# Delta-rule stage of an audio tower: squares on the off-diagonal tiles, two groups' products in one TensorE job, 16 slots instead of 28

## The reference, cut to what matters

```
qkvb = (normed @ W_slow.T).reshape(slen, bsz, H, 5 * D + 2)       # slen 64, bsz 246, H 8, D 64
q, k, v, rk, rv, beta, rbeta = jnp.split(qkvb, ...)
q, k, rk = softmax of each;  beta, rbeta = sigmoid of each
def fw_step(W, inp):                                              # one step of the first recurrence
    qt, kt, vt, bt = inp
    v_old = jnp.einsum('bhij,bhj->bhi', W, kt)
    W = W + (bt * (vt - v_old))[..., :, None] * kt[..., None, :]
    return (W, jnp.einsum('bhij,bhj->bhi', W, qt))
```

## Time and profile before

| what | us |
|---|---|
| time of the kernel, median of 3 runs | 18280.08 (18266.01 to 18282.9) |
| profiled execution, first to last instruction (span) | 18228.0 |
| stage `delta`, first to last instruction | 5642.9 to 9888 of the span |
| PE busy, of the span | 13070.7 (72%) |
| DVE / ACT / POOL busy, of the span | 10572.6 / 6554.5 / 2261.8 |

### The profile page before, as it was taken

The page is one execution under the profiler, slowest core; times in us unless marked ns, Lnnn a source line. Parts: engine busy times, 40 slices in busy tenths (PEclk is TensorE's granted clock), DMA queues, the critical chain, the costliest instruction groups (busy, mean ns, idle before and its releaser), DMA issues. The chain is left out here.

```text
span 18228.0 us, 593330 instructions
## 1 busy us (share of the span) xinstructions
PE 13070.7 (72%) x262069; PEld 10252.8 (56%) x262069; DVE 10572.6 (58%) x24424; ACT 6554.5 (36%) x16019; POOL 2261.8 (12%) x1394
## 2 busy tenths in 40 slices
PE   4607778770866999999997766776677676867777
PEld 3504566660544777777775555555555565645555
DVE  6451457774125666666666777666767645446664
ACT  3101236550213666666664221111112122345541
POOL 0038200003461111111111000000000000000001
PEclk9556568875867999999998766776687697967775
DMA  0313320121332111111112112201220152177652
GB/s 20 110 26 49 72 48 21 34 76 33 72 59 67 28 25 27 28 26 27 27 26 51 21 38 45 44 19 38 45 44 19 38 149 79 45 237 195 193 135 65
DMA packets 1835030, 1095.27 MB, mean 60 GB/s; under 512 B 1109166, under 2 KB 1763409, under 8 KB 1814481
## 3 DMA queue, kind: packets, MB, share of 16 engines
q1 hardware_dynamic: 1605063, 999.32, 22.7%
q0 software_dynamic: 227328, 57.19, 2.1%
HBM read 569.43 MB, written 484.53 MB: 58 GB/s over the span
## 5 line engine op out<-in xcount | busy, mean ns | idle before, releaser
L2894 PE MATMUL recur_acc<-recur_U,recur_W 8*32 8x64 f32 (+4 forms) x49152 | 1406.2, 270 | 504.8 <-ACT recur_W L2816 429.9
L2894 PEld LDWEIGHTS recur_acc<-recur_U,recur_W 8*32 8x32 f32 (+4 forms) x49152 | 1071.1, 140 | 924.5 <-ACT recur_W L2816 741.8
L2945 DVE TENSOR_TENSOR recur_pr<-recur_K,recur_e 124x64 f32<-124x64 f32 (+60 forms) x1024 | 1282.0, 1252 | 395.8 <-ACT recur_e L2828 395.6
L2881 PE MATMUL recur_acc<-recur_R,recur_E 128*32 128x64 f32 x62976 | 1212.6, 233 | 243.2 <-issue 232.7
L2950 DVE TENSOR_REDUCE recur_dot<-recur_pr 124x1 f32<-124x64 f32 (+60 forms) x1024 | 1281.6, 1252 | 29.7
L2881 PEld LDWEIGHTS recur_acc<-recur_R,recur_E 128*32 128x32 f32 x62976 | 1078.3, 118 | 343.5 <-issue 288.1
L2816 ACT ACTIVATE recur_W<-recur_wT 128x256 f32<-128x256 f32 (+16 forms) x1024 | 336.1, 328 | 1969.9 <-PE recur_wT L2866 1968.8
L2866 PE MATMUL recur_wT<-const_ident,recur_w 128*128 128x128 f32 (+15 forms) x1536 | 480.8, 375 | 768.5 <-DVE recur_w L2954 762.1
L2475 ACT ACTIVATE delta_B1l<-delta_pS 64x256 f32<-64x256 f32 x1968 | 745.1, 379 | 704.5 <-PE delta_pS L2375 679.9
L2475 ACT ACTIVATE delta_B0l<-delta_pS 64x256 f32<-64x256 f32 x1968 | 745.6, 379 | 620.9 <-PE delta_pS L2375 600.5
L2510 POOL TENSOR_TENSOR delta_QK<-delta_QK,delta_mx 128x512 f32<-128x512 f32 x369 | 380.3, 1045 | 3038.1 <-DVE delta_mx L2563 3038.0
(11 more groups left out here) (620 smaller groups left out, 33946.8 us busy)
## 6 DMA issues: line engine op xcount, KB each, us to landing
scr<-rel_BD SPq DMA_DIRECT2D x128, 1288.0 KB
rel_sc<-scr SPq DMA_DIRECT2D x128, 861.0 KB
xnT<-ln_xT SPq DMA_DIRECT2D x64, 492.0 KB, 3.0
kr<-delta_QK SPq DMA_DIRECT2D x492, 64.0 KB, 2.3
ur<-delta_Uf SPq DMA_DIRECT2D x492, 64.0 KB, 2.2
zz<-delta_Z SPq DMA_DIRECT2D x492, 64.0 KB, 2.2
recur_K<-kr SPq DMA_DIRECT2D x64, 448.0 KB
recur_H<-zz SPq DMA_DIRECT2D x64, 448.0 KB
```

The lines of the kernel that those rows point to most:

```text
L2881: nc.tensor.matmul(acc[a][32 * q:32 * q + 32, 0:FD], E[a][:, EQ * q + 32 * j:EQ * q + 32 * j + 32], R[a][:, m, :], start=(j == 0), stop=False)
L2894: ins = nc.tensor.matmul(acc[a][32 * q:32 * q + 32, 0:FD], W[a][0:8 * k, b, 160 * q + 32 * j:160 * q + 32 * j + 32], U[a][0:8 * k, 2 * (t ...
L2945: V.tensor_tensor(pr[0:cp, 0:n, :], K[a][0:cp, r0:r0 + n, :], e[a][0:cp, None, :].to_broadcast([cp, n, FD]), ALU.mult).then_inc(s_own[a], 1)
```

## The change

- In `job(one, two)`, which replaces `head`, `tail` and `outer`, the squared transpose goes to the off-diagonal tiles too (into `pS`, now two kinds side by side, 64 columns each), and the applied part alone stays on the diagonal tiles (into `pM`). The tail or the outer product of another group is issued in the same loop, on the diagonal tiles. All products have 64 columns. `outer` of group G - 1 stands in the job of level 3, k = 0.
- A group has 8 jobs, a pair 16 slots, numbered without the empty places. The last slots of a run have tails alone.
- ACT copies both kinds of `pS` at once: two copies of 64 partitions x 512 (64 x 256 at the last level) instead of three copies, and doesn't wait for DVE there.
- The projections stand at slots 0 to 4, each behind that slot's job. The two of values are no longer copied by ACT: DVE scales them from PSUM into a double buffer `V0`, at slots 3 and 4. The other three copies stand in the projection's own slot instead of the next.
- Maxima at slots 1 to 3 (before 2 to 4), exponentials at 3 to 5 (before 5 to 7), sums at 5 to 7 (before 7 to 9), transposes at 8 to 10 (before 16 to 18).
- The key products of both groups go into two PSUM buffers at once, on all four tiles, in three sets (slots 11, 13, 15) instead of six; their masks stand at slots 11 to 15, and set 2 and 3 wait for the masks of the set before.

```diff
-        NM, NG_, NE, NV = 10, 14, 8, 4
-        PROJ_AT = {0: 0, 1: 1, 2: 2, 11: 3, 12: 4}
-        TURN_AT = {16: 0, 17: 1, 18: 2}
-        GRAM_AT = {19: 0, 20: 1, 21: 2, 22: 3, 23: 4, 24: 5}
-        MAX_AT, EXP_AT, SUM_AT = 2, 5, 7
+        NM, NG_, NE, NV = 10, 11, 6, 4
+        NSLOT = 16
+        PROJ_AT = {0: 0, 1: 1, 2: 2, 3: 3, 4: 4}
+        VAL_AT = {3: 0, 4: 1}
+        MAX_AT, EXP_AT, SUM_AT = 1, 3, 5
+        TURN_AT = {8: 1, 9: 2, 10: 0}
+        GRAM_AT = {11: 0, 13: 1, 15: 2}
+        MASK_AT = {11: ((0, 0),), 12: ((0, 1),), 13: ((1, 0),), 14: ((1, 1),), 15: ((2, 0), (2, 1))}
...
-                        for a in range(4):
-                            for h in HALF:
-                                mm(pM[k][h, a, more.start - 1:2, :], now[h, a, 0, :], now[h, a, more, :])
-                            for x, h in enumerate(HALF):
-                                ins = mm(pS[k][HALF[1 - x], a, :], now[h, a, 1, :], now[h, a, 0, :])
...
+                        for a in range(4):
+                            for x, h in enumerate(HALF):
+                                if one and l < SQ - 1:
+                                    mm(pS[k][HALF[1 - x], a, 1, :], now[h, a, 0, :], now[h, a, 1, :])
+                                if one:
+                                    done_one = mm(pM[k][h, a, :], now[h, a, 0, :], u[h, a, :])
+                            for x, h in enumerate(HALF):
+                                if one:
+                                    done_one = mm(pS[k][HALF[1 - x], a, 0, :], now[h, a, 1, :], now[h, a, 0, :])
+                                if two and kind == "tail":
+                                    last = level(k2, G2 % 2, SQ)
+                                    done_two = mm(pT[k2][h, a, :], last[h, a, 0, :], P[k2][h, a, :] if m else last[h, a, 2, :])
+                                elif two:
+                                    done_two = mm(pT[0][h, a, :], az[G2 // 2 % 2][G2 % 2][h, a, :], P[0][h, a, :])
...
                         if n in TURN_AT:
...
+                            if j < 2:
+                                pe.wait_ge(s_v, NV * p + 2 * j + 2)
+                            else:
+                                pe.wait_ge(s_e, NE * p + 4)
                             if j == 0:
                                 pe.wait_ge(s_k, p + 1)
...
                         if n in GRAM_AT:
+                            kind = GRAM_AT[n]
+                            if kind == 0:
+                                pe.wait_ge(s_e, NE * p + 6)
+                            else:
+                                pe.wait_ge(s_m, NM * p + 4 * kind)
                             for a in range(4):
+                                for g in range(2):
+                                    for h in HALF:
+                                        ins = mm(gp[g][h, a * FD:(a + 1) * FD], ...)
...
+                            kinds = slice(0, 2) if l < SQ - 1 else slice(0, 1)
                             for x, h in enumerate(HALF):
-                                ins = nc.scalar.activation(new[h, :, 0, :], pS[k][HALF[1 - x], 0:4, :], ACT.Copy)
-                            if l < SQ - 1:
-                                act.wait_ge(s_dv[k], SQ * G + l + 1)
-                                ins = nc.scalar.activation(new[:, :, 1, :], pM[k][:, :, 0, :], ACT.Copy)
+                                ins = nc.scalar.activation(new[h, :, kinds, :], pS[k][HALF[1 - x], :, kinds, :], ACT.Copy)
                             ins.then_inc(s_ac[k], 1)
...
+                            for g in range(2):
+                                V.tensor_tensor(V0[(p + newer) % 2][k][:, g], vv[:, g], be[:, g].unsqueeze(2).to_broadcast([128, 4, FD]),
+                                                ALU.mult).then_inc(s_v, 1)
```

More of the change, by code:

```diff
@@ L2358, in entries @@
                     for k in range(2):
-                        order.append((G // 2, 14 * (G % 2) + len(order) % 14, ("head", G, x, k)))
-                        if x < TL:
-                            order.append((G // 2, 14 * (G % 2) + len(order) % 14, ("tail", G - 1, x, k) if G else None))
+                        second = None
+                        if G and x < TL:
+                            second = ("tail", G - 1, x, k)
+                        elif G and k == 0:
+                            second = ("outer", G - 1, x, k)
+                        order.append((G // 2, 8 * (G % 2) + 2 * x + k, (G, x, k), second))
             for x in range(TL):
                 for k in range(2):
-                    order.append((pairs, 28, ("tail", 2 * pairs - 1, x, k)))
+                    order.append((pairs, NSLOT, None, ("tail", 2 * pairs - 1, x, k)))
+            order.append((pairs, NSLOT, None, ("outer", 2 * pairs - 1, TL, 0)))
             return order
         def step_of(base, solves, preps):
-            work = entries(solves) if solves else [(0, n, None) for n in range(28)]
+            work = entries(solves) if solves else [(0, n, None, None) for n in range(NSLOT)]
+            newer = 1 if solves else 0
+            rhs = lambda G, l, k: V0[G // 2 % 2][k][:, G % 2] if l == 0 else level(k, G % 2, l)[:, :, 2, :]
             with st.step() as block:
@@ L2427, in _ @@
                     xv = xc[:].rearrange("p a s -> p (a s)")
                     kt = lambda kind, hd: KT[FD * (hd % 2):FD * (hd % 2) + FD, 4 * kind + hd // 2, :]
-                    for p, n, job in work:
-                        if job is not None:
-                            kind, G, x, k = job
-                            (head if kind == "head" else tail)(G, x, k)
-                            if kind == "head" and x == SQ - 1 and k == 0 and G:
-                                outer(G - 1)
-                            if n == 28 and x == TL - 1 and k == 1:
-                                outer(G)
+                    for p, n, one, two in work:
+                        if one or two:
+                            job(one, two)
@@ L2518, in read_head @@
                     def read_head(G, l, k):
[L2519 removed]
+                        u = rhs(G, l, k)
                         dve.wait_ge(s_S[k], SQ * G + l + 1)
@@ L2541, in read_outer @@
                         V.tensor_copy(Z[:, :, G % 2, :], pT[0][:, 0:4, :]).then_inc(s_z, 1)
-                    for p, n, job in work:
+                    for p, n, one, two in work:
                         if n == 0 and p < preps:
-                            new = base + p + (solves > 0)
+                            new = base + p + newer
                             V.tensor_copy(xc[:].rearrange("p a s -> p s a"), X[:, :, bass.ds(2 * new, 2)]).then_inc(s_x, 1)
@@ L2550, in _ @@
                             V.tensor_copy(sb_[p % 2][:], beta[:, bass.ds(new, 1)].rearrange("p n h a -> p (n h) a")).then_inc(s_be, 1)
-                        if job is not None:
-                            kind, G, x, k = job
-                            (read_head if kind == "head" else read_tail)(G, x, k)
-                            if kind == "head" and x == SQ - 1 and k == 1 and G:
-                                read_outer(G - 1)
-                            if n == 28 and x == TL - 1 and k == 1:
-                                read_outer(G)
+                        if one:
+                            read_head(*one)
+                        if two and two[0] == "tail":
+                            read_tail(*two[1:])
+                        elif two:
+                            read_outer(two[1])
                         if p >= preps:
```

137 lines of the change are left out of this document (56 added, 81 removed).

## The result

The changed kernel takes **18642.61 us** (median of 4 runs, 18626.67 to 18645.54), the kernel before 18281.49 beside it (18266.01 to 18284.57): a ratio of 1.0194, 95% interval [1.0181, 1.0206]. It is slower by 361 us; 146 were forecast. The direction, the gap and the fall of the clock came as predicted.

What follows compares the result with a forecast made beforehand. PE's queue was taken to bound the stage, busy 30.99 of 33.10 us a round. 32.1 at full clock plus 2.2 for the clock gave 34.3, 1.2 more x 122 = 146 us: 18425 us, range 18140 to 18750.

Steps and rivals of the forecast that it cites:

- the sum of the round at full clock: New round added slot by slot with PE at full clock: 31.5 us plus 0.6 for seams, 32.1.
- the correction for seams: Old round's priced parts came to 31.7 us, 1.4 under the 33.1 measured; half, 0.6, was added to the new round.
- The clock's term: Half-rate PE work behind each round's gap adds 1.5 to 2.8 us a round, middle 2.2.
- rival 1: Clock holds through each round's gap: -1.0 us a round, 18160; 18050 if DVE reaches the last sum 1.5 sooner; chance 0.19.
- Slots 0 to 4, 2.09 us each: Job 0.93, shape change 0.10 and projection 1.06 in each of the first five slots; ACT and DVE hide.
- The ACT pair, 1.20: ACT's two 512-wide copies reading a job take 2 x 0.60 us, bounds 0.98 to 1.3.
- The chain sum, scales, scaling, transposes: From last sum at 14.84 us, 1.57 to POOL's start, 2.76 scaling, keys ready 19.2, slot 8's transposes start 19.27.
- A gap of 3.5 to 4.5 us released by the scaling: PE idles 4.0 us a round, 15.23 to 19.27, before slot 8's transposes, until POOL's scaling of the keys ends.
- The gap throttles the clock, through J9 or J10: Each round's gap sends PE to 1.2 GHz, at half rate through slot 9's or 10's job; stage clock 0.75 to 0.92.
- Rival 2: Clock stays down until the next round's projections: +7.2 us, 19035; 18650 if down to slot 12 or so; chance 0.16.
- Rival 3: Packing doesn't pay, a job takes 1.33 to 1.39 us: round 35.7 without clock effect, 18597; chance 0.05.
- Rival 4: Both effects cancel, clock falling only in some rounds or for one job: round 33.1, 18280; chance 0.10.

Runs made afterwards that it cites:

- w1: Changed kernel with five full-array products of 256 columns, results unused, put in PE's gap ahead of slot 8's transposes: 18485.51 us, ratio 1.0112.
- u2: Kernel before with a burst of 384 products of 64 columns once a round (slot 14), on all four tiles: 20982.73 us, ratio 1.1483.
- b1: Kernel before with the 128-column products of levels 1 and 2 split into two of 64 columns on the same tiles: 18495.08 us, ratio 1.0114.
- m1: Changed kernel with scaling by thirds, key products merged into two sets, and 128-column diagonal-tile products back in slots 10 to 13: 17893.55 us, 0.9794 of the kernel before.
- t1: Changed kernel with 64 one-column products, results unused, put in PE's gap ahead of slot 8's transposes: 18838.47 us, ratio 1.0303.
- u1: Kernel before with a burst of 384 one-column products once a round (slot 14), on all four tiles: 21249.58 us, ratio 1.1632.

## Where the prediction failed, and what of it held

**The step that failed is the sum of the round at full clock, 31.5 + 0.6 = 32.1 us.** It prices the job by its tiles' pace (0.93), takes the correction for seams by half, and has PE's instructions always there when the array is free: their supply is a term that it puts at nothing without a word. With the clock held up (w1) the round is 35.05: 2.95 more, of which 2.6 are stops. A job has 128 instructions, half a packet, which by the 3.74 us of u2 is 1.87 us of supply for 0.93 of array. Where a projection stands beside it the two together have 2.1 us and 132 instructions, and it mostly goes well; in slots 11 to 15 it can't, and there most of the stopped time lies. The whole round, 2092 instructions, needs 8.2 x 3.74 = 30.6 us of supply against 25.0 before.

**The clock's term was mis-sized the other way**: 2.2 forecast, 1.0 to 1.3 measured, since the lower clock and the short supply partly hide each other (0.6 us of it shows as the stops that w1 adds). Together: 32.1 + 2.2 = 34.3 forecast, 35.05 + 1.03 = 36.08 measured; 1.78 x 122 = 217 us, the whole miss.

**The direction was right by luck in part.** With the clock's measured price, 1.03, the predicted sum gives 33.1 us, no change. That the kernel is slower is the work of the stops, which the sum lacks; the forecast got there by a clock that it priced twice too high.

Point by point. One sum of the prediction is off: rival 1 has 18050 if the last sum comes 1.5 us sooner, where its own terms give 18160 - 1.5 x 122 = 17977.
- *Slots 0 to 4, 2.09 us each*: 2.15 (projections at 5777.40, 5779.54, 5781.69). Right. *The ACT pair, 1.20*: 1.19. Right.

```profile
5777.40 1.12 PE L2379 MATMUL delta_gp<-delta_W,delta_xc 128*128 128x512 f32 x2
...
5779.54 1.13 PE L2379 MATMUL delta_gp<-delta_W,delta_xc 128*128 128x512 f32 x2
...
5781.69 1.13 PE L2379 MATMUL delta_gp<-delta_W,delta_xc 128*128 128x512 f32 x2
```

- *The chain sum, scales, scaling, transposes*: forecast 1.57, then 2.76, transposes 8.82 behind the job of slot 5. Measured 1.57 (5791.36 to 5792.93), 2.76 and 8.79 (5787.04 to 5795.83). Right. *A gap of 3.5 to 4.5 us released by the scaling*: released so, but 3.3, just short; the last job ahead of it started 0.5 later than I had it (5791.36).

```profile
5791.36 0.68 DVE L2577 TENSOR_REDUCE delta_sm<-delta_QK 128x8 f32<-128x512 f32 x1
...
5792.93 2.76 POOL L2514 TENSOR_TENSOR delta_QK<-delta_QK,delta_sm 128x1536 f32<-128x1536 f32 x1 [6.50 <-DVE delta_sm L2586]
...
5795.83 1.09 PE L2458 MATMUL delta_gp<-const_ident,delta_QK 128*128 128x128 f32 x4 [3.31 <-POOL delta_QK L2514]
```

- *The gap throttles the clock, through J9 or J10*: it is at 0.50 until 5801.8, where J10 ends; from 5720 to 9700 the clock is 0.91, inside 0.75 to 0.92. Right, as the earlier trace rows had it; only the price was too high. The stretch in the changed kernel and in w1:

```profile
5720.00:9700.00 3980.00, 3044.24 (x112583) 2366.80 (x112587) 2226.00 (x6026) 2439.08 (x4411) 632.60 (x429) 0.91 0.15 25
...
5720.00:9700.00 3980.00, 3211.78 (x117353) 2481.18 (x117346) 2293.94 (x6220) 2523.47 (x4556) 653.88 (x444) 0.98 0.15 26
```

- *Two more waits for masks of about 1 us*: 0.6 (5806.28 to 5806.87) and 1.0 (5809.68 to 5810.71) in this round. Right.
- *Rival 1* (the clock holds): false, though with the clock held the change would still lose (w1, 1.0112), which this rival did not foresee. *Rival 2* (it stays down): false. The Trainium skill's rule for transposes (TensorE: Matmul & The Clock Gate, "PE-mode transpose") would have kept it down; here it was back at 5801.8, with two sets of transposes and two jobs since the gap. *Rival 3* (packing doesn't pay): its size, 35.7 us, was near the truth for a wrong reason. It looked for the price in the array, at 1.33 to 1.39 a job; a job that is not stopped takes 0.98 up to the next job (5787.04 to 5788.02) and 1.1 up to a projection, so 0.93 was nearly right for the array. *Rival 4*: false.
- The correction of 1.4 us for seams in the old round was the one number that pointed at something unpriced, and I halved it because it was unexplained. b1 shows that the old round's last slots already stood near the edge of the supply. But stops take only 0.1 us a round there, so supply doesn't account for the 1.4 as idle time; its cause stays open.

**Open**: why packets are never less than some 3.3 us apart in the bursts when each is on its way for 1.1. And the remaining 0.3 us between 2.95 and the stops.

## What to carry to other kernels

Count instructions beside columns: for each stretch of a few microseconds, PE instructions (weight loads and both float32 passes counted) x 14.6 ns (u2's mean) against its array time; the larger one is the first estimate of its price. The supply theory's ranges, worked out much like this, missed by up to 0.8 us a round (b1), since it matters in which stretch the instructions stand. Splitting wide products to fill small tiles pays beside long ones and costs beside other short ones, so choose it slot by slot, as m1 does. And an idle time of PE "for nothing that the profile shows", in mid-job, is worth a look at the instruction queue's packets before the clock is blamed.

## What the hardware showed that was not expected

- A sustained supply of 14.6 ns per PE instruction (3.74 us for 256), against an issue pace of 7.5 ns while there is stock; 465 instructions in 3.50 us, nearly two packets' worth, ran before the first stop of the burst shown (in the 122 bursts of u2 272 to 684, median 416).
- A stop ends 1.2 to 1.6 us behind the landing of a packet: 261 of 267 in the changed kernel, 310 of 310 in w1.
- Array work in a 3.3 us gap holds the clock (5 products of 256 columns, 128 x 128); 64 one-column products there don't (t1). In bursts of one-column products the clock falls from 1.00 and stays at 0.5 (u1), where bursts of as many products of 64 columns, behind the same wait, keep it at 1.00 (u2).
